# Global attention: the causal triangle zeroed in the exponentials by GpSimd instead of bias products on TensorE

## The reference

```python
q, k, v = (proj(Wq, bq), proj(Wk, bk), proj(Wv, bv))        # tanh(states @ W + b)
alpha = jnp.einsum('bhqd,bhkd->bhqk', q, k) / jnp.sqrt(jnp.float32(d))
causal = jnp.tril(jnp.ones((s, s), dtype=bool))
alpha = jnp.where(causal, alpha, jnp.finfo(jnp.float32).min)
alpha = jax.nn.softmax(alpha, axis=-1)
ctx = jnp.einsum('bhqk,bhkd->bhqd', alpha, v)
```

## Time and profile before

| | us |
|---|---|
| median of the runs | 2591.67 |
| the profiled execution | 2589.23 |
| its span, first to last instruction | 2587.4 |
| PE busy | 2381.7 |
| DVE busy | 1919.3 |
| ACT busy | 1543.3 |
| POOL busy | 618.5 |

### The profile page before, as it was taken

One profiled execution on the slowest core, in us unless ns is written; L12 is line 12 of the kernel. 1 busy time (PEld: TensorE's weight loads), 2 busy tenths in 40 slices (PEclk: granted clock), 3 DMA queues, 4 the chain that ended last, 5 costly groups with the idle time before them and its releaser, 6 DMA issues. The chain is left out here.

```text
span 2587.4 us, 65680 instructions
## 1 busy us (share of the span) xinstructions
PE 2381.7 (92%) x21336; PEld 1898.6 (73%) x21336; DVE 1919.3 (74%) x4552; ACT 1543.3 (60%) x3026; POOL 618.5 (24%) x711
## 2 busy tenths in 40 slices
PE   5999899999999995299999998999799999998995
PEld 4767667767777774288888886888588888886884
DVE  6999699879969994567777776666477777765666
ACT  4777477667747773266666665344366666664442
POOL 1000000000000000444444444212344444442222
PEclk8999999999999998599999999999899999998998
DMA  3100100010001003100000000100100000001003
GB/s 110 39 18 12 56 19 12 29 46 16 15 6 52 12 18 113 64 1 0 8 0 8 1 8 3 48 0 0 45 0 7 1 8 0 8 0 51 0 0 130
DMA packets 70204, 62.43 MB, mean 24 GB/s; under 512 B 3972, under 2 KB 67196, under 8 KB 69760
## 3 DMA queue, kind: packets, MB, share of 16 engines
q1 hardware_dynamic: 70144, 61.66, 7.5%
HBM read 49.05 MB, written 8.40 MB: 22 GB/s over the span
## 5 line engine op out<-in xcount | busy, mean ns | idle before, releaser
L511 ACT ACTIVATE at_p<-at_ps_s,at_shift 128x1024 f32<-128x1024 f32 (+3 forms) x384 | 336.1, 900 | 85.6 <-PE at_ps_s L680 48.8
L311 DVE TENSOR_TENSOR at_p_lo<-at_p,at_p_hi 128x1024 f16<-128x1024 f32 (+3 forms) x384 | 357.2, 951 | 5.5
L1228 ACT ACTIVATE ly_probs<-ly_masked,ly_small,ly_rq 128x256 f32<-128x256 f32 x512 | 302.2, 592 | 40.0 <-DVE ly_small L1421 40.0
L1640 PEld LDWEIGHTS ly_ps<-ly_values,ly_probs_T 128*128 128x128 f32 x2048 | 248.3, 191 | 48.7 <-issue 48.7
L1640 PE MATMUL ly_ps<-ly_values,ly_probs_T 128*128 x2048 | 269.5, 274 | 12.6 <-ACT ly_probs_T L1236 12.6
L1418 DVE CUSTOM_DVE_ANT_0 ly_masked<-ly_ps,ly_mask 128x256 f32<-128x256 f32 x520 | 199.7, 421 | 91.5 <-PE ly_ps L1621 90.9
L1236 ACT ACTIVATE ly_probs_T<-ly_ps 128x512 f32<-128x512 f32 x256 | 151.9, 594 | 178.8 <-PE ly_ps L1630 131.2
L1118 POOL TENSOR_TENSOR ly_rope_a<-ly_rope_a,ly_rope_t 128x512 f32<-128x512 f32 x132 | 169.2, 1282 | 304.1 <-DVE ly_rope_t L1391 304.1
L708 PE MATMUL at_ps_o<-at_v,at_p_hi 128*128 128x65 f16 x2304 | 237.7, 193 | 0.0
L709 PE MATMUL at_ps_o<-at_v,at_p_hi 128*128 128x64 f16 x2304 | 236.8, 194 | 0.0
L708 PEld LDWEIGHTS at_ps_o<-at_v,at_p_hi 128*128 128x128 f16 x2304 | 210.6, 96 | 34.5 <-issue 25.7
(11 more groups left out here) (232 smaller groups left out, 6303.0 us busy)
## 6 DMA issues: line engine op xcount, KB each, us to landing
ly_a_raw<-in_ffn_wqkv SPq DMA_DIRECT2D x3, 1536.0 KB, 6.4
at_w_raw<-in_Wv SPq DMA_DIRECT2D x34, 128.0 KB, 2.2
at_w_raw<-in_Wq SPq DMA_DIRECT2D x34, 128.0 KB, 2.3
at_w_raw<-in_Wk SPq DMA_DIRECT2D x34, 128.0 KB, 2.3
at_xio<-in_states SPq DMA_DIRECT2D x4, 1024.0 KB, 6.0
x<-at_xio SPq DMA_DIRECT2D x4, 1024.0 KB, 4.4
stream<-x SPq DMA_DIRECT2D x4, 1024.0 KB, 9.6
out_x<-x SPq DMA_DIRECT2D x4, 1024.0 KB, 10.3
```

The source lines that it names most:

```text
L311: dve.tensor_tensor(p_lo[u % P_RING][:, :, off:], probs[u % P_RING][:, :, off:], p_hi[u % P_RING][:, :, off:], ALU.subtract).then_inc(p_lo ...
L511: act.activation(probs[u % P_RING][:, :, off:], ps_s[u % 2][:, :, off:], ACT.Exp, bias=shift[:], scale=SCORE_SCALE).then_inc(exp_done, 1)
L1228: step = act.activation(pr[:, j % 2, h, :], sm[:, j % 2, h, :], ACT.Exp, bias=small[:, j % 2, 1, h:h + 1], scale=rq[:, par, 2 * j + h:2 * ...
L1640: step = pe.matmul(ps_pv[:, cols], pT[:, (2 * slot + h) * P:(2 * slot + h + 1) * P], vv[:, v_slots[slot], cols], start=(j == 0 and h == 0 ...
```

## The change

The 8 bias steps per pair go from TensorE, and with them the table `at_causal` and its load. In their place GpSimd runs one `affine_select` for each diagonal unit, after its exponential and in place on `at_p`: of the 2x128x128 block on the diagonal it keeps the elements whose query is not before their key and writes 0.0 over the others. Each is one instruction over 128 partitions x 256 float32 elements. `high_probs` of a diagonal unit now waits for `masked` in place of `exp_done`, and `sc_done` is signalled by the last score product of the unit itself.

```diff
-        causal = a.sb("at_causal", [P, P], F16)
...
-                sp.dma_start(causal[:], io["causal16"]).then_inc(ld_const, 16)
...
+                def causal_masks(it):
+
+                    for u in filter(diagonal, range(NU)):
+                        off = unit_offset(u)
+                        block_of = probs[u % P_RING][:, :, off:off + P]
+                        hold(pool, tick, (exp_done, at(it * NU + u + 1)))
+                        pool.affine_select(block_of, block_of, [[0, 2], [1, P]], ALU.is_ge, 0.0, base=0,
+                                           channel_multiplier=-1).then_inc(masked, 1)
...
-                for b in range(2, B):
-                    inverse_deviations(b)
+                for b in range(B):
+                    with pool.Fori(0, HP) as j:
+                        causal_masks(b * HP + j)
+                    if b + 2 < B:
+                        inverse_deviations(b + 2)
...
                 def high_probs(it, u):
                     off = unit_offset(u)
-                    dve.wait_ge(exp_done, at(it * NU + u + 1))
+                    if diagonal(u):
+                        dve.wait_ge(masked, it * NDIAG + nth_masked(u))
+                    else:
+                        dve.wait_ge(exp_done, at(it * NU + u + 1))
                     dve.wait_ge(pv_done, at(it * NU + u + 1 - P_RING))
...
                         score_products(par, u)
-                    for u in units:
-                        if diagonal(u):
-                            causal_bias(u)
...
                             step = pe.matmul(ps_s[u % 2][:, h, off:], kx[rows, keys], qx[rows, cols], start=(n == 0),
-                                             stop=(n == 2 and not diagonal(u)), skip_group_check=True)
-                    if not diagonal(u):
-                        step.then_inc(sc_done, 1)
-
-                def causal_bias(u):
-                    off = unit_offset(u)
-                    for h in range(2):
-                        step = pe.matmul(ps_s[u % 2][:, h, off:off + P], ident16[:], causal[:], start=False, stop=True,
-                                         skip_group_check=True)
+                                             stop=(n == 2), skip_group_check=True)
                     step.then_inc(sc_done, 1)
```

More of the change, by code:

```diff
@@ L141, in phase_modulation_and_attention @@
         ps_m16 = [m[:].bitcast(F16).rearrange("p (t h d) -> p t h d", t=TB, h=2) for m in ps_m]
-        (ld_const, ld_wo, ld_w, ld_x, st_x, const_done, wo_done, sc_done, pv_done, pj_mm, vt_mm, ct_mm, op_mm, yt_mm,
+        (ld_const, ld_wo, ld_w, ld_x, st_x, masked, const_done, wo_done, sc_done, pv_done, pj_mm, vt_mm, ct_mm, op_mm, yt_mm,
          exp_done, pj_full, vt_hi, ct_hi, y_done, p_hi_done, pj_hi, wh_done, p_lo_done, pj_lo, wl_done, r_done, cx_done,
          vt_lo, ct_lo, yg_done, x1_done, tick) = a.sems(
-            "at_", "ld_const ld_wo ld_w ld_x st_x const_done wo_done sc_done pv_done pj_mm vt_mm ct_mm op_mm yt_mm "
+            "at_", "ld_const ld_wo ld_w ld_x st_x masked const_done wo_done sc_done pv_done pj_mm vt_mm ct_mm op_mm yt_mm "
             "exp_done pj_full vt_hi ct_hi y_done p_hi_done pj_hi wh_done p_lo_done pj_lo wl_done r_done cx_done "
@@ L194, in unit_offset, with diagonal, nth_masked @@
             return max(0, kt * P - qc * CH)
+        def diagonal(u):
+            qc, kt = UNITS[u]
+            return kt * P >= qc * CH
+        NDIAG = sum(1 for u in range(NU) if diagonal(u))
+        def nth_masked(u):
+            return sum(1 for i in range(u + 1) if diagonal(i))
         def o_view():
@@ L557, in _ @@
                 stream_hi(0, 1)
-                act.wait_ge(ld_const, 16 * 4)
+                act.wait_ge(ld_const, 16 * 3)
                 for i in range(NPJ):
@@ L661, in scores @@
                         score_products(par, u)
-                    for u in units:
-                        if diagonal(u):
-                            causal_bias(u)
-                def diagonal(u):
-                    qc, kt = UNITS[u]
-                    return kt * P >= qc * CH
                 def score_products(par, u):
@@ L765, in _ @@
                         stream_T(1, 1)
-                pe.wait_ge(ld_const, 16 * 4)
+                pe.wait_ge(ld_const, 16 * 3)
                 pe.wait_ge(pj_hi, at(NPJ))
@@ L772, in _ @@
                 score_products(0, 0)
-                causal_bias(0)
                 pe.wait_ge(ld_rows, 16)
@@ L1779, in constants @@
         "ident16": np.eye(P, dtype=np.float16),
-        "causal16": np.where(q >= k, 0.0, -60000.0).astype(np.float16),
         "rope": rope_tables(),
```

## The result

The changed kernel takes 2609.18 us (median of 4 runs, 2607.75 to 2610.98) against 2592.12 us for the kernel before (4 runs). The ratio is 1.0068, with a 95% interval of 1.0050 to 1.0085: slower by 17 us. The forecast of a loss was right; its size, 80 us, was nearly five times too large.

A forecast was written before the change was run, and what follows sets the result against it. TensorE sets the pace at 25.94 us a pair, VectorE close behind. VectorE's 24.98 us plus (M + 0.12) + 7 (M - 0.21) gives 28.43 us at M = 0.60, 80 us slower over 32 pairs: 2672 us, range 2600 to 2800 us.

The forecast's parts named there:

- The bound and the ceiling: TensorE sets the pace, VectorE one microsecond behind; removing 16 bias products a pair could gain 0.96 us, 31 us in all.
- The price of one mask: Duration M of one GpSimd select on 128x256 float32: taken as 0.60 us, with ends 0.40 and 1.65 us.
- the sum: Time of a head pair: 24.98 + (M + 0.12) + 7 (M - 0.21) = 23.63 + 8 M, 28.43 us at M = 0.60.
- The lower end: M = 0.40 us, the plain GpSimd copy of the same elements: a pair of 26.83 us, 28 us of loss.
- the wait before unit 0: VectorE waits for mask 0 before unit 0's cast, including the ways to and from GpSimd: M + 0.12 us a pair.
- The collision: GpSimd masks and VectorE's casts, low parts and splits exclude each other: M - 0.21 us for each of seven masks.
- VectorE's floor: VectorE's own work for a head pair, 25.94 us less 0.96 us of idle time: 24.98 us.
- Moving masks earlier than VectorE's need: The seven masks other than unit 0's: their exponentials come ahead of VectorE's need, so no waiting for a result is charged.
- No collision: Rival: masks do not hold up VectorE; a pair of 25.70 us, 8 us faster, 2584 us; chance 0.09.
- Balance: Rival: M near 0.3 us, or collisions for one or two masks alone; within 0.2%, 2592 us; chance 0.05.
- A mask that gets no turn: Rival: masks wait until VectorE stands still; pair 30.74 us, 154 us slower, 2745 us; chance within the forecast's.
- Few collisions: Rival: only about three of seven masks meet an excluded VectorE instruction; pair 26.87 us, 30 us slower, 2622 us; chance 0.06.

The follow-up runs named there:

- spare-tile kernel: Changed kernel with the same select on a spare tile and VectorE not waiting for it (triangle not zeroed): 2591.36 us, ratio 0.9997.
- the fifth mask: Unit 2's mask added to the batched-bias kernel with masks on units 3, 8, 9 and 10, VectorE's low 1 moved ahead of high 2: 2591.07 us, ratio 0.9998.

## Why the prediction was right in sign and wrong in size

**The bound and the ceiling: right.** Two nearly full engines, and 31 us at stake on TensorE: the kernel with neither bias nor mask is 29 us faster. The clock stayed at 1.00, as the loop's busy times after show.

**The price of one mask: the step that failed.** The prediction took M = 0.60 us, "nearer to the addition" than to the 0.40 us copy. It is 0.41 us undisturbed: the copy. The least durations for 256 and 128 elements, 0.406 and 0.292 us, differ by 0.9 ns an element, against 0.83 ns between the 0.40 us copy and the 0.19 us cast of two elements; computing the condition costs nothing that shows. Since the sum multiplies M by eight, this one term is, in the sum, 8 x 0.19 = 1.52 us a pair and 49 us of the 63 us by which 2672 us missed 2609 us. The prediction's estimate from the Trainium skill (GPSIMD Engine Reference, section 3.1, about 1.8 cycles per element) gave 0.57 us and misses in the same way. The same section also puts a short loop body at 1.03 cycles per element; worked out in the same way that would be 0.41 us, an estimate on which the measured duration lies, and the prediction left it out. The lower end, 0.40 us, was stated, and with it 2620 us; the choice between the ends was the error, not the range, in which 2609 us lies.

**The sum: near in total, not confirmed in form.** With M = 0.41 us it gives 23.63 + 3.28 = 26.91 us against the 26.60 us measured, some 0.3 us too high. Term by term: the wait before unit 0 was to be M + 0.12 = 0.53 us, and is 0.61 us (0.56 us in the other pairs): the way back from GpSimd took 0.14 us (412.09 to 412.23 us) and not 0.05 us. The collision was to be M - 0.21 = 0.20 us for each of seven masks, and is 0.20 us where casts or low parts follow each other directly (0.89 to 1.09 us, 1.55 to 1.75 us), but only 0.07 us where a low part waits for its own cast anyway (1.23 to 1.30 us): the mask slips into that gap. Mask 8 lengthens no VectorE row: it is held up by low 7 and shows as the wait of 0.30 us. The rest is VectorE's floor. The prediction subtracted the idle times of the earlier trace rows alone; but a wait also costs the 0.08 us by which VectorE's instructions otherwise overlap, four times over, so that the floor was nearer to 24.7 us than to 24.98 us. The spare-tile kernel, in which VectorE hardly waits, says the same: its rows are lengthened by 1.34 us a pair over the kernel with neither, and 26.05 - 1.34 = 24.7 us. These two are the 10 us that remain, with 3 us for a pair of 26.04 us and not 25.94 us before. The form itself, 8 M, is not what the runs show: a pair moved by 0.57 of it between 0.29 and 0.41 us, and by 0.92 of it when every mask was doubled, but there mostly by waits that the sum did not charge.

**Moving masks earlier than VectorE's need: right for the changed kernel, and not in general.** The sum charged no waiting to masks 1 to 3 and 9 to 11. So it was, because VectorE was already late by mask 0's wait. In the kernel with biases on units 0 and 8 waits for masks 1, 2 and 11 appeared in its place; with half masks, which make VectorE less late, those for masks 2 and 11; and with doubled masks, which come later themselves, those for masks 1, 2, 10 and 11.

**The rivals.** No collision is refuted by the select on the spare tile: 29 us. Balance near M = 0.29 us: the select over half the elements takes 0.29 us, and its kernel ties with the one before, ratio 1.0000. That the two meet there is in part luck, since the slope of 8 on which the point rests is only 0.57 of itself on this side (0.92 on the other, for another reason). A mask that gets no turn is refuted by the masks that start within a cast and end 0.7 us later. "Few collisions" named 2622 us and three free masks, at M = 0.60 us; none of the seven was free: six lengthen a VectorE row, two of them by 0.07 us only, and mask 8 is waited for.

**What stays open.** How long a pair is at other lengths of the mask can't be read from the sum, since each length moves the waits. No kernel in which TensorE's bias sits on units 0 and 8 without the cost of its place between the units was run, so the price of mask 0's wait alone is not known. Nor was the fifth mask tried without the changed order.

## What to carry to other kernels

Work moved from the fullest engine to an idle one can still cost the second fullest: count on that engine what the new helper takes from it, here 0.2 us of VectorE for each 0.12 us of TensorE, and let the helper take only pieces whose result isn't needed at once, and no more than bring the two to the same length (four of eight won 0.5% where eight lost 0.7%, but three won under 0.2% and five nothing). Where a price is multiplied by the number of pieces, settle it before anything else: this one-input GpSimd operation took what a copy of the same size takes. Don't extend a sum of waits and collisions to other lengths without looking where the waits go: taking one away lets the next appear. And read an idle time with the overlap that it also destroys, and a pair's length from several pairs.

## What the runs showed of the hardware

A GpSimd select of float32 takes 0.41 us for 256 and 0.29 us for 128 elements per partition. Beside a GpSimd memset VectorE's double-rate casts grow (552 to 629 ns on average for 128x768) and its two-input subtractions do not (951 and 948 ns); beside a select both do (646 and 1042 ns). A select of 0.41 us costs VectorE 0.20 us where its instructions follow each other without a gap, and one of 0.29 us 0.09 us (the two casts behind it take 0.98 us in place of 0.89 us). On TensorE two 128-row products between score products on 64 rows take 0.21 us to the next start where they take 0.12 us with other 128-row products around them, and a step with them in its middle is 0.21 us longer as a whole.
